# A transformer layer on one core: a small indirect DMA into the gather buffer, then a clear of that buffer

## The reference

```python
xn = layernorm(x)
x = x + gnn_attention(xn, edges) + linear_attention(xn)
xt = layernorm(x)
gates = sigmoid(xt @ expert_sel.T)              # 384 x 32 experts
sel_val, sel_idx = top_k(gates, 4)              # each token goes to 4 experts
scores = relu(einsum('nd,edf->nef', xt, keys))  # keys 32 x 1024 x 512
scores = scores * gate_full[:, :, None]
x = x + einsum('nef,efv->nv', scores, values)   # values 32 x 512 x 1024
```

## Time and profile before

| | |
|---|---|
| runs | 803.19, 803.78, 804.21 us; median 803.78 us |
| profiled execution | span 802.0 us from the first to the last instruction; its end-to-end time is not recorded by itself |
| TensorE | 779.0 us busy, 97% of the span |
| VectorE, ScalarE, GpSimd | 400.1, 246.1, 194.7 us busy |
| granted TensorE clock | 0.999 of full speed |
| DMA | 207.10 MB, some 425 GB/s in the expert stage |

### The profile page before, as it was taken

The page is one execution under the profiler, slowest core; times in us unless marked ns, Lnnn a source line. Parts: engine busy times, 40 slices in busy tenths (PEclk is TensorE's granted clock), DMA queues, the critical chain, the costliest instruction groups (busy, mean ns, idle before and its releaser), DMA issues.

```text
span 802.0 us, 11580 instructions
## 1 busy us (share of the span) xinstructions
PE 779.0 (97%) x4187; PEld 544.5 (68%) x4187; DVE 400.1 (50%) x887; ACT 246.1 (31%) x427; POOL 194.7 (24%) x215
## 2 busy tenths in 40 slices
PE   6999999999999999999999998999999999999997
PEld 6997889988998999997557753444444444444433
DVE  6579976754443336446873784233223332322234
ACT  4553421242332233337882231211111121111111
POOL 2126344544434430006890000100000001000000
PEclk9999999999999999999999999999999999999999
DMA  8962534233333443421107899999999999999936
GB/s 316 411 266 106 199 118 158 72 140 106 129 136 105 158 165 109 154 105 54 54 2 286 344 350 370 423 426 425 425 426 426 426 424 426 423 428 426 424 132 261
DMA packets 35606, 207.10 MB, mean 258 GB/s; under 512 B 7812, under 2 KB 8196, under 8 KB 12256
## 3 DMA queue, kind: packets, MB, share of 16 engines
q1 hardware_dynamic: 27648, 191.00, 59.7%
q0 software_dynamic: 7184, 14.71, 4.9%
q10 hardware_dynamic: 720, 0.68, 0.2%
HBM read 204.91 MB, written 4.43 MB: 261 GB/s over the span
## 4 chain that ended last, share of the span: by engine, by line
PE 81%; DMA 9%; DVE 5%; issue 1%; ACT 1%; SPq 1%; POOL 1%; DVEq 0%; POOLq 0%; ACTq 0%
PE ps L1636 22%; PE ps L1358 14%; PE ps L1359 14%; PE ps L1360 14%; DMA ring<-in_keys 4%; DMA raw<-in_keys 3%; PE ps L1676 3%; PE ps L1677 2%; PE ps L499 2%; PE ps L1648 2%; PE ps L1719 1%; PE ps L488 1%; DMA etmp<-xt_dram,gidx 1%; PE ps L473 1%; DVE wl L978 1%
## 5 line engine op out<-in xcount | busy, mean ns | idle before, releaser
L978 DVE TENSOR_TENSOR wl<-raw,wh 128x1024 fp32r<-128x1024 f32 x87 | 107.3, 1235 | 123.8 <-ACT wh L781 123.1
L781 ACT ACTIVATE wh<-raw 128x1024 fp32r<-128x1024 f32 x88 | 93.0, 1061 | 193.6 <-PE ps L1360 191.8
L709 POOL DMA_INDIRECT plane<-code,idx x96 | 95.1, 991 | 119.2 <-DMA plane<-code,idx 92.8
L1318 DVE TENSOR_TENSOR acc<-ps,acc 128x512 f32<-128x512 f32 x102 | 62.5, 681 | 101.6 <-PE ps L1677 101.6
L1636 PE MATMUL ps<-ring,hT 128*64 128x512 f32 x424 | 103.2, 596 | 0.7 <-ACT hT L901 0.7
L1636 PE MATMUL ps<-ring,xgT 128*64 128x512 f32 x376 | 100.6, 593 | 2.3 <-DMA ring<-in_keys 2.3
L1358 PE MATMUL ps<-xnh,wh 128*128 128x384 f32 x256 | 87.0, 340 | 0.2 <-DVE xnl L1093 0.2
L1359 PE MATMUL ps<-xnl,wh 128*128 128x384 f32 x256 | 86.6, 338 | 0.0
L1360 PE MATMUL ps<-xnh,wl 128*128 128x384 f32 x256 | 86.4, 338 | 0.0
L1313 DVE TENSOR_TENSOR yl<-ps,yh 128x512 fp32r<-128x512 f32 x34 | 23.5, 691 | 99.7 <-ACT yh L907 99.7
L1636 PEld LDWEIGHTS ps<-ring,xgT 128*64 128x64 f32 x376 | 32.1, 137 | 57.4 <-issue 52.0
(11 more groups left out here) (267 smaller groups left out, 1397.5 us busy)
## 6 DMA issues: line engine op xcount, KB each, us to landing
ring<-in_values SPq DMA_DIRECT2D x53, 1024.0 KB, 23.1
ring<-in_keys SPq DMA_DIRECT2D x49, 1024.0 KB, 21.6
raw<-in_keys SPq DMA_DIRECT2D x19, 1024.0 KB, 18.1
raw<-in_values SPq DMA_DIRECT2D x11, 1024.0 KB, 25.2
raw<-in_w_v SPq DMA_DIRECT2D x8, 1024.0 KB, 4.8
raw<-in_w_q SPq DMA_DIRECT2D x8, 1024.0 KB, 4.8
raw<-in_w_k SPq DMA_DIRECT2D x8, 1024.0 KB, 4.7
key_rows<-key_dram POOLq DMA_DIRECT2D x6, 1024.0 KB, 8.2
```

What stands on the lines that cost most here:

```text
L709: nc.gpsimd.indirect_dma_start(plane[m], bass.IndirectOffsetOnAxis(idx[:, g:g + 1].bitcast(U32), 0), code[:, g:g + 1], None, bounds_check= ...
L781: nc.scalar.activation(wh[:, s % SUB], raw[:, c % RAW, 2 * (s % 2):2 * (s % 2) + 2, :], ACT.Copy)\
L978: nc.vector.tensor_tensor(wl[:, s % SUB], raw[:, (s // 2) % RAW, 2 * (s % 2):2 * (s % 2) + 2, :], wh[:, s % SUB].bitcast(F32), ALU.subtrac ...
L1318: nc.vector.tensor_tensor(rows_of, ps[bank], rows_of, ALU.add).then_inc(s_add, 1)
```

## The change

GpSimd gets four steps between L732 and the clear of `xg`: it clears the one-column index tile `gcol[0]`, waits for that, issues an indirect DMA that reads 8 words (32 bytes) for each of 128 lanes, all from the first words of the input `x` since every index is 0, into the first 8 columns of `xg`, and waits until this DMA has landed. Only then is `xg` cleared, as before. Nothing of it is used: the clear overwrites it.

```diff
+WORDS = 8
...
+        s_column = sem("s_column")
+        s_ahead = sem("s_ahead")
...
             nc.gpsimd.tensor_scalar(small[:, 0, :], cst["iota"][:, 0:NE], FIXED - 0.5, None, ALU.is_ge).then_inc(s_movable, 1)
+            nc.gpsimd.memset(gcol[0][:, :], 0).then_inc(s_column, 1)
+            pool.wait_ge(s_column, 1)
+            nc.gpsimd.indirect_dma_start(xg[:, 0:WORDS], None, x.rearrange("n (a b) -> (n a) b", b=WORDS),
+                                         bass.IndirectOffsetOnAxis(gcol[0][:, :].bitcast(U32), 0),
+                                         bounds_check=N - 1, oob_is_err=False).then_inc(s_ahead, 16)
+            pool.wait_ge(s_ahead, 16)
             nc.gpsimd.memset(xg, 0.0).then_inc(s_pch, 1)
             pool.wait_ge(s_pch, 1)
             pool.wait_ge(s_xtd, 16 * NT)
```

## The result

The changed kernel took 806.01 us in the median of 8 runs (803.91 to 806.75), the kernel before 803.58 (803.16 to 804.91) beside it: a ratio of 1.0026, 95% interval [1.0016, 1.0036]. It is 2.4 us slower, 2.3 above the forecast of 803.7 and outside its range. The profiled execution took 806.68 us with a span of 804.9, 2.9 above the span of before; the mean granted clock was 0.994.

The account below looks back on a forecast made before the run. TensorE, fed at the loads' rate from 520 us, bounds the kernel, with a 2.0 us stall behind the first gather. First use saves 0.09 us, all else 0: -0.1, span 801.9, time 803.7 us; range 802.5 to 804.9.

Parts of the forecast that it names:

- The wait for it ... Cost on the path 0: GpSimd's wait for the small DMA: only the buffer clear and first gather stand behind it, so cost 0.
- I take 0: Moved clear, at 461.4 to 462.4 us on VectorE's scaling of the last rows: expected to cost nothing.
- the cover that the prediction counted: GpSimd's idle time before the first gather: 17.5 us left after the clear, 9.4 with the 10.3 us landing.
- Landing of the small DMA: Small DMA from 459.24 us: taken to land 2.2 us after its start, at 461.4; 10.3 as the other end.
- the clear collides: Rival, chance 0.12: clear delays VectorE's second scaling operation, 0.56 us, at most 0.96; time 804.3, at most 804.7.
- The prediction's first paragraph: What bounds the kernel: a microsecond TensorE loses or gains at 490 us moves the end by about one.
- The first gather is slow because of VectorE: First gather's 1.96 us descriptor writing: blocked by VectorE's two-input operation, done about 0.93 us after that ends.
- The gain of the first use: First gather's descriptor writing: the small DMA ahead of it saves 0.09 us of first use.
- the first use really costs: Rival, chance 0.11: first use makes the gather slow; it lands 0.9 to 1.9 us sooner, 801.8 to 802.9.
- The wait outlasts its cover: Rival, chance 0.03: small DMA lands too late for the first gather, 4.2 us late if queued; 808.0.
- The stall's bound: TensorE's 2.0 us stall before its transposes is all that a change on the first gather can win.
- The 6 us for a first call: Skill's hidden cost of a first call into a freshly loaded library; the prediction saw nothing hidden before the gather.

Follow-up runs that it names:

- r3_late_clear: Kernel before, no small DMA, with the clear of the buffer waiting for the last scaled rows; ratio 1.0012 [1.0002, 1.0022].
- r10_late_clear_again: Kernel before, no small DMA, with the clear held back until the last scaled rows, a second time; ratio 1.0008 [0.9999, 1.0017].
- r9_after_fourth: The changed kernel, unedited, loaded and compared a fourth time with the kernel before; ratio 1.0013 [1.0003, 1.0022].
- r4_tables_wait: Kernel before, with VectorE's two seat-table comparisons held back until the first gather is issued; ratio 0.9997 [0.9988, 1.0006].
- r12_early_best: Changed kernel with the small DMA at 422 us, the seat-table comparisons held back and filler matmuls on TensorE; ratio 0.9992 [0.9982, 1.0001].
- r11: Changed kernel with the small DMA and its wait moved to 422 us, the clear back at 458.4; ratio 0.9997 [0.9987, 1.0007].
- r15_clear_ahead_again: Changed kernel with the clear moved to 421 us and the small DMA left in its place, second load; ratio 1.0012 [1.0003, 1.0021].
- r8_filler: Kernel before with the seat-table comparisons held back and four filler matmuls on TensorE around the first hidden values' transposes; ratio 0.9991 [0.9982, 1.0000].

## Why the prediction was wrong

**The step that failed** is the zero for what the small DMA and its wait do to the way to the table: "The wait for it ... Cost on the path 0", and for the moved clear "I take 0". GpSimd's own path had the cover that the prediction counted; what was late were two steps of other engines, 0.55 us at the logit parts and 0.54 at the gates, and the table came 1.10 us late. Three terms were wrong.

1. *Landing of the small DMA*: taken as 2.2 us from the first scatter, measured 3.4 to 3.7 in the traces with it at 459 to 461 us. The bounds named (2.2 and 10.3) held it; the value taken put the clear at 461.4 to 462.4, on the row scaling, and in truth it ran at 462.5 to 464.3, beside the gates or just behind them.
2. *The collision*: the rival "the clear collides" had the mechanism and a price (0.56, at most 0.96 us), on the wrong operation. It hits L1195, with no idle time behind it, and costs 0.38 to 0.68 us (0.58 to 0.88 less 0.20), shown without the small DMA by r3_late_clear and r10_late_clear_again. It had 0.12, because "nothing in the trace shows a clear that stretches VectorE", which was an absence of rows and not a row. The section of the Trainium skill that the prediction cited (SBUF — State Buffer, Who interferes with whom) also says that a `tensor_scalar` can enter a two-port mode, and that whoever issues first then gets the shared pair of ports for the whole instruction, while the other blocks fully. These traces agree, in that the gates end 0.04 to 0.06 us after the clear in each of the six hits; whether L1195 is in such a mode no row says.
3. *The late logit parts*, 0.53 to 0.58 us, were in no case of the prediction. They stand in four of the six traces of the changed kernel, and, with 0.64 and 0.65 us, in both with the clear taken away. Without them the clear of the changed kernel misses: gates on time run from 4.80 to 5.00 us after the small clear, and the clear starts at 4.96 to 5.31. So in the changed kernel the collision hangs on the late parts, and the forecast came out in two comparisons of five (803.90 and 804.05 us, both well inside its range; r9_after_fourth is at its upper edge with 804.87). Which kind of load the first comparison would meet, nothing beforehand told.

In the first comparison 2 and 3 add up to the 1.10 us of the table. The prediction's first paragraph has a microsecond at 490 us move the end by about one, either way. For a loss the first profile agrees (2.23 us at the transposes, none of it won back); for a gain the runs don't: 1.0 us sooner in r4_tables_wait gave 0.2 us, 1.6 sooner in r12_early_best gave 0.6, at most 1.4 by the interval. From the transposes to the end the profiled executions take anything from 311.5 to 313.8 us, a spread as large as the effect. The remaining 1.3 us of the 2.4 are not shown piece by piece. In the profiled execution the lower clock accounts for 0.8. Over the timed runs the mean granted clock is 0.9958 in the first comparison, 0.9957, 0.9958, 0.9955 and 0.9960 in the other four with late parts, and 0.9973 and 0.9971 in the two without (the kernel before beside the later ones: 0.9968 to 0.9978). A difference of 0.0015 is 1.2 us of TensorE's work (0.0015 of 803), or 2.4 us more at half speed. TensorE is idle 0.94 to 1.05 us ahead of L1558 where it was 0.4, which may be what makes such falls likelier; that is argued, not tried, and r3_late_clear has 0.9962 with the parts on time.

**What was right.** The first gather is slow because of VectorE: 1.15 us with the comparisons held back (1.056 is a later gather's), 1.87 with the small DMA ahead and the comparisons there. The gain of the first use is 0.09 us in every trace of the changed kernel (1.87 or 1.88 against 1.96), so the rival "the first use really costs" is out. "The wait outlasts its cover" is out too: 17.2 of GpSimd's 20.7 us of idle time are left. The stall's bound held: even 1.6 us sooner at the transposes (488.65 against 490.26) did not give a time that the measurement tells from before. The 6 us for a first call that the prediction quoted from the Trainium skill (GPSIMD Engine Reference, Instruction dispatch) show in no run here.

**What stays open.** Why the parts are late in four comparisons and not in two. Both kinds came on two of the chips, so it isn't the chip alone; all changed kernels of one comparison behaved alike. The traces of the comparisons with late parts have 3,650 to 3,773 signals recorded before 450 us, the others 3,973 to 3,978, and r10, r11 and r12, in which nothing critical falls on descriptor writing, have the low counts too, so something is different in those loads well before the small DMA comes; by itself it costs nothing that these three runs tell from the kernel before. What it is, and why just these signals of TensorE come late in them, no run here told.

## What to carry to other kernels

Before a GpSimd clear or an indirect DMA is moved, list what VectorE and TensorE do in the microseconds where it will land, and take the landing time with its error: the cover of 17 us on GpSimd's own path was real, and the price was paid by two neighbours. An operation which "writes nothing that is read" is not free if it sits inside the chain of another engine; here the same small DMA at 422 us cost nothing and at 459 us between nothing and 0.26%. And a first gather that seems slow should be held against the two-input operations of VectorE beside it before a warm-up is built for it.

## What the runs showed that was not expected

- A GpSimd clear of 128x1024 blocks a VectorE TENSOR_SCALAR over 128x64 float32 until it ends (0.58 to 0.88 us in place of 0.20), but not a RECIPROCAL over the same tile (0.55 us beside it and without).
- In four of six loads of the changed kernel the signal behind the first logit parts, which falls into the writing of the small DMA's descriptors, comes only 0.16 to 0.20 us after the writing's end; the matmuls are issued on time, and the signals inside the writing of the scatters are not late (50 of 50 in r15_clear_ahead_again).
- The clock falls to 1.2 GHz for 3.4 or 6.8 us between 462 and 492 us in some executions, of the kernel before too; with four more matmuls in TensorE's idle time (r8_filler) all 11 runs had a mean clock of 0.998 or more.
- The small DMA, 128 reads of 32 bytes with the DMA engines nearly idle (share 0.13 at 460 to 462 us), took 3.4 to 3.7 us to land, the first scatter 2.2.
